# A two-layer gated cross-attention and mixture-of-experts block: Newton steps of seven layer norm chains on VectorE, and later gathers for chunks 5 to 7

## The chip, the cores and the metric

The kernel runs on one core of a Trainium2 chip. The metric is device time of one execution in microseconds, lower is better. The engines are named as the profile names them: PE (TensorE), DVE (VectorE), ACT (ScalarE), POOL (GpSimd) and SP (SyncE, which here issues DMAs). Each engine works through its own instructions strictly in the order in which they are written, and waits on semaphores for the others.

## The reference, cut to what matters

There are 32 sequences of 128 rows with 128 features, and two layers. Each layer is a cross-attention over 120 context rows with 16 heads, and a mixture of 8 experts of which each row takes two. Ahead of each of the four stands a layer norm without weights.

```python
def _layernorm(x, axis=-1, eps=1e-05):
    m = jnp.mean(x, axis=axis, keepdims=True)
    v = jnp.var(x, axis=axis, keepdims=True)
    return (x - m) / jnp.sqrt(v + eps)
...
x = x + jnp.tanh(g_xattn[0]) * _L0_xattn_ref(_layernorm(x, axis=-1), ctx_1024, ctx_1024, fside_BxSxS2_0, mask, ...)
x = x + jnp.tanh(g_ffn[0]) * _L0_ffn_ref(_layernorm(x, axis=-1), ...)
x = x + jnp.tanh(g_xattn[1]) * _L1_xattn_ref(_layernorm(x, axis=-1), ctx_1024, ctx_1024, mask, ...)
x = x + jnp.tanh(g_ffn[1]) * _L1_ffn_ref(_layernorm(x, axis=-1), ...)
```

The experts of layer 0 have a capacity: each row is sent to a place in its expert's table, the experts run over the tables, and the results are gathered back to the rows. The experts of layer 1 have none; each expert runs over all rows and its result is weighted.

## The kernel before

**Tiling.** The 32 sequences (rows 0 to 31 of `x_rows`, each 128x128) are worked in 8 chunks of 4 (`NCH`, `CB`). A chain of a layer norm is named by two numbers, `(who, n)`: `who` is 0 ahead of an attention and 1 ahead of the experts, `n` is the chunk, with 8 added in layer 1. Chunk 1 of layer 1, `n` = 9 (`HALVED`), is done in two halves of two rows each.

**The slots.** An attention is a walk over slots `s` = 0 to 139 or so: four per row, and in each a group of four heads passes through scores (PE), maxima (DVE, L986), exponentials (ACT, L805), their turn (PE, L529), the copy of the turned ones (DVE, L996 or L998; ACT takes one in four in layer 1), and later the weighted sums (PE, L542). Everything else is put by hand between these, by tables of offsets: `NEAR1`, `MID1`, `FAR1` and `FAR2` say at which slot of layer 1 the next chunk's statistics (`stat`), its root (`power`), its normalising (`norm`), its turn on PE (`turn`), its projection and the split of its queries stand; `POST` and `TIGHT0` say the same for what follows an attention chunk, the routing of the experts among it. DVE carries out, in a slot, first its `early` part, then its attention part, then its `behind` part. POOL has only `behind` and one small copy (L1426) every fourth slot.

**A layer norm chain.** DVE makes the statistics (L968, L972). POOL adds the epsilon (L1390), takes the power of minus one half (L1392), and refines it by one Newton step in four operations, then makes the shift `-m*r` in two (L1395 to L1405). Then the rows are normalised, `x*r + (-m*r)`, by POOL (L1418) or, for seven chains, by DVE (L1116): `(0, 8)`, both halves of `(0, 9)`, `(0, 10)`, `(0, 11)`, `(1, 6)` and `(1, 7)`. PE turns them (L463). In all seven, the slot of `norm` is later than the slot of `power`, by two or three; the chains `(0, 8)` and the first half of `(0, 9)` lie in the expert stage of layer 0.

**The gathers.** POOL also sends the rows to the tables (L1480, layer 0, `send`) and asks for the results (L1499, `bring`): two gathers a row, one in each of two slots, starting with slot `bring_slot(i)`. DVE adds them to the row at slot `add_y_slot(i)` (L1101, L1103), with rows 16 to 19 at slots 29 to 32, 20 to 23 at 38 to 41, 24, 25, 26, 27 at 50, 52, 54, 56 and 28 to 31 at 66, 68, 70, 72. The gathers of rows 24 to 27 began at slots 37, 39, 41, 43, those of rows 28 to 31 at 52, 54, 56, 58.

**The keys.** Behind the attention of layer 0, DVE splits the keys of layer 1 into three bf16 parts (L1165, L1167, L1169), for key chunks 0 and 1 at offset 2 of the last chunk, for chunk 2 at offset 5. `norm` of `(1, 7)` stands at offset 4, the logits (L1028) at 13. The experts of layer 0 begin when the last of the sends has landed.

Of the kernel before, what the change touches and what calls it, by code (L numbers as in the profile page):

```python
# [19 lines left out]
CB = 4  # L20
# [83 lines left out]


class Waits:

# [48 lines left out]
def bring_slot(i):  # L156

    c, b = divmod(i, CB)
    return {8: 0, 9: 7, 10: 9, 11: 11}[i] if c == 2 else {3: 13, 4: 21, 5: 29, 6: 37, 7: 52}[c] + 2 * b

# [28 lines left out]

SPLIT_KEYS_AT = {2: (0, 1), 5: (2,), 19: (3, 4, 5)}  # L190

# [26 lines left out]
def flamingo(nc, t, out, scratch):  # L218
# [193 lines left out]
    def ln_slot(who, n):  # L412
        return 0 if who == 0 else 1 + n % 2
# [540 lines left out]
    def vector_program(dve):  # L954
# [144 lines left out]
        def add_y(i):  # L1099
# [3 lines left out]
            dve.scalar_tensor_tensor(x[:, i, :], got[:, i % RING_Y, 1, :], slot_w[:, 1, i:i + 1], x[:, i, :], ALU.mult, ALU.add).then_inc(combine, 1)  # L1103

        def normalise_rows(who, n, c, h=0):
            if who:
# [8 lines left out]
            for b in part_of(None if who else n, h)[1]:  # L1115
                dve.tensor_scalar(xn[:, ln_slot(who, n), b, :], x[:, c * CB + b, :], rs[:, who, 2, b:b + 1], rs[:, who, 3, b:b + 1], ALU.mult, ALU.add).then_inc(ln_norm[who], 1)  # L1116

# [69 lines left out]
        def behind(l, s):  # L1187
# [11 lines left out]
            for P in range(1, NCH):  # L1199
                o, C, at = s - start_slot(l, P), l * NCH + P, prep_at(l, P)  # L1200
                if o == at["stat"]:
                    stat_rows(0, C, l, P)
                if l == 1 and P in ON_DVE1:
                    if o == at["norm"]:
                        normalise_rows(0, C, P)
# [6 lines left out]
            for j in range(NCH):  # L1212
                o, n = s - after_slot(j), l * NCH + j
                if o == post_at(l, j)["stat"]:
                    stat_rows(1, n, l, j)
                if l == 0 and j >= ON_DVE and o == post_at(l, j)["norm"]:
                    normalise_rows(1, j, j)
# [61 lines left out]
        def experts0():  # L1279
# [3 lines left out]
            for n in range(NJ):  # L1283
# [6 lines left out]
                if n == ADD_LAST:  # L1290
                    add_y(CB - 1)
                    stat_rows(0, NCH, 1, 0)
                if n == NORM_FIRST:
                    normalise_rows(0, NCH, 0)
                if n == SPLIT_FIRST:
# [3 lines left out]
                if n == ADD_NEXT:  # L1299
                    for i in range(CB, EARLY_ROWS):  # L1300
                        add_y(i)
                    stat_rows(0, HALVED, 1, 1, 1)
                if n == NORM_NEXT:
                    normalise_rows(0, HALVED, 1, 1)
# [72 lines left out]
    def gpsimd_program(pool):  # L1377
# [5 lines left out]
        def powers(who, n, h=0):  # L1383
# [7 lines left out]
            on.wait_ge(power, 2 * m + 1)  # L1391
            pool.tensor_tensor(r_s[:, 0, :], r_s[:, 4, :], half_c[:, 0:p], ALU.pow).then_inc(power, 1)  # L1392
            y, t_, r, m_r = (r_s[:, j, :] for j in range(4))
            on.wait_ge(power, 2 * m + 2)
# [528 lines left out]
```

## Time and profile before

| what | value |
|---|---|
| median of three runs | 959.44 us (957.41 to 962.17) |
| the profiled execution | 961.64 us |
| its span | 959.8 us |
| busy: PE, DVE, ACT, POOL | 793.3, 670.6, 608.5, 571.8 us |
| mean granted clock of PE | 0.941 of 2.4 GHz |

The span runs from the first to the last instruction; 1.8 us of the profiled execution lie around it. The stages are: attention of layer 0 up to 300 us, routing and keys up to 333, experts of layer 0 up to 463, attention of layer 1 up to about 730, experts of layer 1 to the end. The bracket at the end of a row of the view in order of time is the time for which the engine stood idle ahead of the instruction, and what ended it; a row without one began when the engine was free. Engines overlap neighbouring instructions a little, so what counts is from start to start.

### The profile page before, as it was taken

Reading aid. Unit: us, or ns where it says so; the run is one execution under the profiler, and the core shown is the slowest. Engines: PE = TensorE matmul, PEld = TensorE weight load, DVE = VectorE, ACT = ScalarE, POOL = GpSimd, SP = SyncE. Lnnn points to the kernel's source line nnn. Section 1 sums busy time; section 2 is a strip of 40 time slices with the busy share of each in tenths; the row PEclk is TensorE's granted clock in tenths of the full one; section 3 lists DMA queues with packets and bytes.
Section 4 is the critical chain, followed back from the end, with each engine's and each line's share of the span. In section 5 each row is a group of like instructions: output and inputs, shape, how many; then the busy total and the mean of one; then the engine's idle time right before and its main releaser. Section 6 shows DMA issues by size and latency. Waiting matters only on the chain.

```text
span 959.8 us, 20423 instructions
## 1 busy us (share of the span) xinstructions
PE 793.3 (83%) x6554; PEld 627.5 (65%) x6554; DVE 670.6 (70%) x1933; ACT 608.5 (63%) x2582; POOL 571.8 (60%) x872
## 2 busy tenths in 40 slices
PE   2268898988886399999876788788986889999996
PEld 1146666766664299998555556656765767888885
DVE  1246889999896534436688799998896575666664
ACT  1366888998982255444787678889996344444442
POOL 6364567888777500223477887574341767777775
PEclk9978999999996699999999889999998899999998
DMA  7929789536633742322537367454300000000000
GB/s 172 243 87 242 197 218 274 138 98 157 128 86 130 259 138 83 85 82 85 110 85 140 72 127 173 112 109 120 89 13 24 22 23 23 21 15 14 8 12 22
DMA packets 83699, 101.68 MB, mean 106 GB/s; under 512 B 8289, under 2 KB 69926, under 8 KB 82665
## 3 DMA queue, kind: packets, MB, share of 16 engines
q1 hardware_dynamic: 79496, 92.13, 37.4%
q0 software_dynamic: 4096, 8.25, 3.5%
q8 instruction: 52, 0.85, 0.4%
q14 instruction: 55, 0.44, 0.2%
HBM read 63.32 MB, written 45.99 MB: 114 GB/s over the span
## 4 chain that ended last, share of the span: by engine, by line
PE 41%; DVE 22%; ACT 14%; POOL 9%; issue 9%; DMA 5%; SPq 0%; POOLq 0%; ACTq 0%; DVEq 0%
ACT exp L805 10%; PE psum L654 7%; PE psum L691 5%; PE psum L693 5%; PE psum L692 5%; DVE shift L986 5%; DVE exp_T L996 2%; PE psum L542 2%; PE psum L529 2%; PE psum L642 2%; DVE ln_stats L968 2%; PE psum L643 2%; PE psum L644 2%; DVE exp_T L998 2%; PE psum L707 1%
## 5 line engine op out<-in xcount | busy, mean ns | idle before, releaser
L805 ACT ACTIVATE exp<-psum,shift 128x120 f32<-128x120 f32 x1024 | 364.8, 427 | 92.9 <-DVE shift L986 92.5
L805 ACT ACTIVATION_READ_ACCUMULATOR exp<-psum,shift 128x1 f32 x1024 | 269.8, 273 | 0.0
L986 DVE TENSOR_REDUCE shift<-psum 128x4 f32<-128x480 f32 x256 | 164.9, 646 | 55.4 <-PE psum L520 54.8
L529 PE MATMUL psum<-ident,exp 128*120 128x128 f32 x1024 | 164.5, 285 | 35.1 <-DVE exp_T L998 22.0
L1569 POOL TENSOR_TENSOR q_operand<-q_operand 128x512 f32<-128x512 f32 x96 | 125.9, 1311 | 70.3 <-DVE q_operand L1345 66.1
L1345 DVE SCALAR_TENSOR_TENSOR q_operand<-psum,comb,q_operand 128x256 f32<-128x256 f32 x256 | 111.7, 479 | 79.9 <-ACT q_operand L933 79.9
L529 PEld LDWEIGHTS psum<-ident,exp 128*120 128x120 f32 x1024 | 120.4, 143 | 53.9 <-DVE exp_T L998 26.5
L933 ACT ACTIVATE q_operand<-psum 128x512 f32<-128x512 f32 x128 | 76.4, 598 | 122.3 <-PE psum L693 122.2
L1499 POOL DMA_INDIRECT got_rows<-scratch_y,slot_get x64 | 66.9, 1046 | 121.9 <-DMA scratch_y<-y_rows 104.5
L517 PE MATMUL psum<-neg_rows,const_bf 128*128 128x480 bf16 x256 | 98.7, 386 | 48.4 <-ACT exp L805 27.5
L691 PE MATMUL psum<-w_T_high,xn_T_high 128*128 128x512 f32 x256 | 108.8, 425 | 9.5 <-DVE w_T_low L1311 7.3
L693 PE MATMUL psum<-w_T_high,xn_T_low 128*128 128x512 f32 x256 | 102.5, 400 | 0.0
L692 PE MATMUL psum<-w_T_low,xn_T_high 128*128 128x512 f32 x256 | 102.1, 399 | 0.0
L520 PE MATMUL psum<-k_operand,q_operand 128*128 128x240 bf16 x512 | 98.2, 275 | 0.0
L996 DVE TENSOR_TENSOR exp_T<-psum,group_T 120x512 f32<-120x512 f32 x128 | 85.1, 666 | 1.2 <-PE psum L529 1.2
L517 PEld LDWEIGHTS psum<-neg_rows,const_bf 128*128 128x128 bf16 x256 | 26.6, 104 | 79.7 <-ACT exp L805 49.8
L520 PEld LDWEIGHTS psum<-k_operand,q_operand 128*128 128x128 bf16 x512 | 51.7, 101 | 37.9 <-issue 10.9
L542 PE MATMUL psum<-exp_T,v_spread 120*32 120x128 f32 x2048 | 75.3, 292 | 0.7 <-POOL v_spread L1426 0.7
L1480 POOL DMA_INDIRECT scratch_xe<-xn_rows,slot_put x64 | 64.9, 1014 | 18.5 <-issue 17.4
L654 PE MATMUL psum<-w,q_operand 128*128 128x128 f32 (+1 forms) x576 | 69.1, 275 | 0.0
L654 PEld LDWEIGHTS psum<-w,q_operand 128*128 128x128 f32 (+1 forms) x576 | 66.9, 184 | 1.6 <-issue 0.7
L998 DVE COPY exp_T<-psum 120x512 f32<-120x512 f32 x96 | 65.2, 679 | 0.7 <-PE psum L529 0.7
(164 smaller groups left out, 1557.5 us busy)
## 6 DMA issues: line engine op xcount, KB each, us to landing
k_operand<-scratch_k SPq DMA_DIRECT2D x32, 360.0 KB, 6.3
q_operand<-scratch_q SPq DMA_DIRECT2D x30, 384.0 KB, 6.1
scratch_q<-parts SPq DMA_DIRECT2D x15, 384.0 KB
scratch_k<-parts SPq DMA_DIRECT2D x14, 360.0 KB, 5.2
scratch_xe<-in_zero_rows SPq DMA_DIRECT2D x8, 512.0 KB, 12.6
scratch_y<-in_zero_rows SPq DMA_DIRECT2D x8, 512.0 KB, 6.9
scratch_q<-parts SPq DMA_DIRECT2D x15, 256.0 KB
scratch_k<-parts SPq DMA_DIRECT2D x14, 240.0 KB, 5.3
```

Of the source, the lines that this page charges most:

```text
L517: pe.matmul(bank, ident_b, atts[l].neg[:, k, bb:bb + 1, :].broadcast_to([S, 4, S2]), start=True, stop=False)
L520: ins = pe.matmul(bank[:, 2 * u:2 * u + 2, :], qop[:, C % RING, pt, b * S:(b + 1) * S], kop[:, C % RING, pt, :, b * S2:(b + 1) * S2], star ...
L529: ins = pe.transpose(ps[0:S2, T_BANKS[G % 2], u * S:(u + 1) * S], atts[l].expS[:, G % RING_E, u, :], ident[:, :])
L654: ins = pe.matmul(bank[0:r_, s_ * D:(s_ + 1) * D], hT[:, n % 2, q, s_ * 128:s_ * 128 + r_], w2[:, e_, q, :], start=(q == 0), stop=(q == NC ...
L691: pe.matmul(bank, xh[:, c % 2, rows], vh[:, e_, :], start=True, stop=False)
L692: pe.matmul(bank, xh[:, c % 2, rows], vl[:, e_, :], start=False, stop=False)
L693: pe.matmul(bank, xl[:, c % 2, rows], vh[:, e_, :], start=False, stop=True).then_inc(f_up, 1)
L805: ins = act.activation(atts[l].expS[:, G % RING_E, u, :], ps[:, S_BANKS[G % 3], u * S2:(u + 1) * S2], ACT.Exp, bias=atts[l].shift[:, i % 2 ...
L986: dve.tensor_reduce(atts[l].shift[:, i % 2, 4 * r:4 * r + 4], ps[:, S_BANKS[G % 3], 0:4 * S2].rearrange("p (h k) -> p h k", h=4), AX_X, AL ...
L996: dve.tensor_tensor(dst, src, att0.gT[:, c % 2, b:b + 1, :].broadcast_to([S2, 4, S]), ALU.mult).then_inc(taken_v, 1)
L1345: dve.scalar_tensor_tensor(dst[:, half], ps[:, 2 * (w % R_UP) + k, 0:HID1], comb[:, c, b, 2 * p + k:2 * p + k + 1], sg[:, w % R_SG, half], ...
L1569: pool.tensor_tensor(acc[:, i % R_ACC, :], acc[:, i % R_ACC, :], ga[:, m % R_GA, :], ALU.add).then_inc(f_sum, 1)
```

## The change

The last part of the root moves to DVE for the seven chains whose rows DVE normalises. POOL still adds the epsilon and takes the power, and then stops; six operations of it go away in each chain. DVE gets three: `t = y*y`, `t = (v*-0.5)*t`, `r = (t+1.5)*y`. The shift `-m*r` goes away: the rows are normalised as `(x-m)*r`, in one operation of the same shape.

The new function `roots` waits for POOL's power. It is called at the slot of `power`, not at that of `norm`. In the expert stage it stands directly ahead of the normalising of `(0, 8)`, and directly behind the statistics for the first half of `(0, 9)`.

The gathers of chunk 5 are asked for one slot later (from slot 30), those of chunk 6 eight slots later (from 45), and those of chunk 7 eight slots later (from 60). The slots at which DVE adds them stay. The splits of keys 0 and 1 go from offset 2 to 5, behind the normalising of `(1, 7)`, and those of key 2 from 5 to 8.

```diff
+NEWTON_ON_DVE = [(0, NCH), (0, NCH + 1), (0, NCH + 2), (0, NCH + 3), (1, NCH - 2), (1, NCH - 1)]
+
+def newton_on_dve(who, n):
+    return (who, n) in NEWTON_ON_DVE
...
-    return {8: 0, 9: 7, 10: 9, 11: 11}[i] if c == 2 else {3: 13, 4: 21, 5: 29, 6: 37, 7: 52}[c] + 2 * b
+    return {8: 0, 9: 7, 10: 9, 11: 11}[i] if c == 2 else {3: 13, 4: 21, 5: 30, 6: 45, 7: 60}[c] + 2 * b
...
-SPLIT_KEYS_AT = {2: (0, 1), 5: (2,), 19: (3, 4, 5)}
+SPLIT_KEYS_AT = {5: (0, 1), 8: (2,), 19: (3, 4, 5)}
...
+        def roots(who, n, h=0):
+            p = CB // 2 if h else CB
+            r_s, m_v = rs[:, who, :, 0:p], mv[:, who, 0:p, :]
+            power, rstd, m = (h_pow, h_rstd, 0) if h else (ln_pow[who], ln_rstd[who], n)
+            y, t_, r, v = (r_s[:, j, :] for j in (0, 1, 2, 4))
+            on.wait_ge(power, 2 * m + 2)
+            dve.tensor_tensor(t_, y, y, ALU.mult).then_inc(rstd, 1)
+            on.wait_ge(rstd, 6 * m + 1)
+            dve.scalar_tensor_tensor(t_, v, -0.5, t_, ALU.mult, ALU.mult).then_inc(rstd, 1)
+            on.wait_ge(rstd, 6 * m + 2)
+            dve.scalar_tensor_tensor(r, t_, 1.5, y, ALU.add, ALU.mult).then_inc(rstd, 4)
...
-                dve.tensor_scalar(xn[:, ln_slot(who, n), b, :], x[:, c * CB + b, :], rs[:, who, 2, b:b + 1], rs[:, who, 3, b:b + 1], ALU.mult, ALU.add).then_inc(ln_norm[who], 1)
+                dve.tensor_scalar(xn[:, ln_slot(who, n), b, :], x[:, c * CB + b, :], mv[:, who, b, 0:1], rs[:, who, 2, b:b + 1], ALU.subtract, ALU.mult).then_inc(ln_norm[who], 1)
...
                 if l == 1 and P in ON_DVE1:
+                    if o == at["power"]:
+                        roots(0, C)
                     if o == at["norm"]:
                         normalise_rows(0, C, P)
...
+                if l == 0 and j >= ON_DVE and o == post_at(l, j)["power"]:
+                    roots(1, j)
                 if l == 0 and j >= ON_DVE and o == post_at(l, j)["norm"]:
                     normalise_rows(1, j, j)
...
                 if n == NORM_FIRST:
+                    roots(0, NCH)
                     normalise_rows(0, NCH, 0)
...
                     stat_rows(0, HALVED, 1, 1, 1)
+                    roots(0, HALVED, 1)
...
             pool.tensor_tensor(r_s[:, 0, :], r_s[:, 4, :], half_c[:, 0:p], ALU.pow).then_inc(power, 1)
+            if newton_on_dve(who, n):
+                return
```

Where it moves instructions, first DVE in the attention of layer 1, chain `(0, 11)`, slots 24 to 26, before:

```order
L972 BN_AGGR ln_mean_var<-ln_stats 128x2 x4
L986 TENSOR_REDUCE shift<-psum 128x4
L998 COPY exp_T<-psum 120x512
L1023 SCALAR_TENSOR_TENSOR x_rows<-psum,tanh_g_xattn,x_rows 128x512
L986 TENSOR_REDUCE shift<-psum 128x4
L1003 RECIPROCAL inverse<-den 128x16
L1009 COPY inverse_spread<-inverse 128x128
L1116 TENSOR_SCALAR xn_rows<-x_rows,ln_rstd 128x128 x4
```

and with the change (`L980` is `L972` of before, `L994` is `L986`, `L1137` is `L1116`):

```order
L980 BN_AGGR ln_mean_var<-ln_stats 128x2 x4
L1120 TENSOR_TENSOR ln_rstd<-ln_rstd 128x4
L1122 SCALAR_TENSOR_TENSOR ln_rstd<-ln_rstd 128x4
L1124 SCALAR_TENSOR_TENSOR ln_rstd<-ln_rstd 128x4
L994 TENSOR_REDUCE shift<-psum 128x4
L1006 COPY exp_T<-psum 120x512
L1031 SCALAR_TENSOR_TENSOR x_rows<-psum,tanh_g_xattn,x_rows 128x512
L994 TENSOR_REDUCE shift<-psum 128x4
L1011 RECIPROCAL inverse<-den 128x16
L1017 COPY inverse_spread<-inverse 128x128
L1137 TENSOR_SCALAR xn_rows<-x_rows,ln_mean_var,ln_rstd 128x128 x4
```

The three root steps stand directly behind the statistics, so two maxima, one copy of turned exponentials and one addition of the attention's output, which stood ahead of the first wait for POOL, now stand behind it.

Second DVE behind the attention of layer 0, chain `(1, 7)`, before (L1165 to L1169 are the splits of keys, L1133 ends the routing of chunk 6):

```order
L1133 TENSOR_TENSOR slot_weight<-r_gate,r_tmp 128x4 x2
L1165 TENSOR_TENSOR full<-full,parts 128x480
L1167 CAST parts<-full 128x480
L1169 TENSOR_TENSOR parts<-full,parts 128x480
L1165 TENSOR_TENSOR got_rows<-got_rows 128x480
L1167 CAST got_rows<-got_rows 128x480
L1169 TENSOR_TENSOR got_rows<-got_rows 128x480
L1116 TENSOR_SCALAR xn_rows<-x_rows,ln_rstd 128x128 x4
L1165 TENSOR_TENSOR full<-full,parts 128x480
```

and with the change:

```order
L1154 TENSOR_TENSOR slot_weight<-r_gate,r_tmp 128x4 x2
L1120 TENSOR_TENSOR ln_rstd<-ln_rstd 128x4
L1122 SCALAR_TENSOR_TENSOR ln_rstd<-ln_rstd 128x4
L1124 SCALAR_TENSOR_TENSOR ln_rstd<-ln_rstd 128x4
L1137 TENSOR_SCALAR xn_rows<-x_rows,ln_mean_var,ln_rstd 128x128 x4
L1186 TENSOR_TENSOR full<-full,parts 128x480
L1188 CAST parts<-full 128x480
L1190 TENSOR_TENSOR parts<-full,parts 128x480
L1186 TENSOR_TENSOR got_rows<-got_rows 128x480
```

The normalising has moved ahead of all three splits of keys; before, it stood behind two of them.

Third POOL in the attention of layer 1, slots 28 to 31, from the end of the chain `(1, 8)` to the normalising of its rows, before (L1499 is a gather, L1448 adds a bias):

```order
L1405 TENSOR_TENSOR ln_rstd<-ln_rstd 128x4
L1499 DMA got_rows<-scratch_y,slot_get 128x128
L1448 TENSOR_TENSOR x_rows<-x_rows,bo_rows 128x512
L1499 DMA got_rows<-scratch_y,slot_get 128x128
L1448 TENSOR_TENSOR x_rows<-x_rows,bo_rows 128x512
L1499 DMA got_rows<-scratch_y,slot_get 128x128
L1418 TENSOR_SCALAR xn_rows<-x_rows,ln_rstd 128x128 x4
```

and with the change:

```order
L1434 TENSOR_TENSOR ln_rstd<-ln_rstd 128x4
L1477 TENSOR_TENSOR x_rows<-x_rows,bo_rows 128x512
L1528 DMA got_rows<-scratch_y,slot_get 128x128
L1477 TENSOR_TENSOR x_rows<-x_rows,bo_rows 128x512
L1528 DMA got_rows<-scratch_y,slot_get 128x128
L1447 TENSOR_SCALAR xn_rows<-x_rows,ln_rstd 128x128 x4
```

One gather of three is gone from ahead of the normalising.

## Rows read from the trace of the kernel before

**Rows 1.** The page, the chain of work that ended last, by engine.

```profile
PE 41%; DVE 22%; ACT 14%; POOL 9%; issue 9%; DMA 5%; SPq 0%; POOLq 0%; ACTq 0%; DVEq 0%
```

**Rows 2.** Stretches of layer 1: length, busy time and count by engine, clock, DMA.

```profile
490.00:530.00 40.00, 27.71 (x294) 20.75 (x290) 32.60 (x91) 27.73 (x141) 30.34 (x49) 0.91 0.63 121
530.00:560.00 30.00, 22.35 (x196) 16.36 (x184) 24.77 (x60) 20.87 (x101) 25.92 (x39) 0.84 0.39 94
```

**Rows 3.** DVE in order of time, end of layer 0: start, length, engine, line.

```profile
283.71 0.62 DVE L986 TENSOR_REDUCE shift<-psum 128x4 f32<-128x480 f32 x1
...
289.65 1.12 DVE L1116 TENSOR_SCALAR xn_rows<-x_rows,ln_rstd 128x128 f32<-128x128 f32 x4 [1.94 <-POOL ln_rstd L1405]
```

**Rows 4.** POOL in order of time, the two chains at the end of layer 0.

```profile
286.83 1.05 POOL L1392 TENSOR_TENSOR ln_rstd<-ln_rstd,minus_half 128x4 f32<-128x4 f32 x1
...
302.92 1.05 POOL L1392 TENSOR_TENSOR ln_rstd<-ln_rstd,minus_half 128x4 f32<-128x4 f32 x1
...
318.36 0.97 POOL L1480 DMA_INDIRECT scratch_xe<-xn_rows,slot_put  x1 [1.03 <-DVE slot_weight L1133]
```

**Rows 5.** DVE in order of time, behind the attention of layer 0.

```profile
304.60 0.65 DVE L1165 TENSOR_TENSOR full<-full,parts 128x480 f32<-128x480 f32 x1
...
308.01 1.11 DVE L1116 TENSOR_SCALAR xn_rows<-x_rows,ln_rstd 128x128 f32<-128x128 f32 x4
...
313.00 0.19 DVE L1028 COPY r_logits<-psum 128x32 f32<-128x32 f32 x1 [2.18 <-PE psum L563]
```

**Rows 6.** DVE in order of time, attention of layer 1.

```profile
473.89 0.62 DVE L986 TENSOR_REDUCE shift<-psum 128x4 f32<-128x480 f32 x1
...
475.38 0.42 DVE L1142 TENSOR_TENSOR full<-full,parts 128x256 f32<-128x256 f32 x1 [0.27 <-ACT parts L777]
...
491.59 0.66 DVE L978 TENSOR_TENSOR v_rows<-psum,bv_rows 120x512 f32<-120x512 f32 x1
...
495.15 1.14 DVE L1116 TENSOR_SCALAR xn_rows<-x_rows,ln_rstd 128x128 f32<-128x128 f32 x4
...
502.35 1.50 DVE L1101 SCALAR_TENSOR_TENSOR x_rows<-got_rows,slot_weight,x_rows 128x128 f32<-128x128 f32 x1
...
511.51 0.63 DVE L986 TENSOR_REDUCE shift<-psum 128x4 f32<-128x480 f32 x1
...
516.24 1.11 DVE L1116 TENSOR_SCALAR xn_rows<-x_rows,ln_rstd 128x128 f32<-128x128 f32 x4 [1.86 <-POOL ln_rstd L1405]
...
529.50 0.35 DVE L1101 SCALAR_TENSOR_TENSOR x_rows<-got_rows,slot_weight,x_rows 128x128 f32<-128x128 f32 x1 [3.65 <-DMA got_rows<-scratch_y,slot_get]
...
532.49 0.35 DVE L1101 SCALAR_TENSOR_TENSOR x_rows<-got_rows,slot_weight,x_rows 128x128 f32<-128x128 f32 x1 [0.48 <-DMA got_rows<-scratch_y,slot_get]
```

**Rows 7.** POOL in order of time, attention of layer 1.

```profile
474.39 1.04 POOL L1392 TENSOR_TENSOR ln_rstd<-ln_rstd,minus_half 128x4 f32<-128x4 f32 x1
...
492.09 1.05 POOL L1392 TENSOR_TENSOR ln_rstd<-ln_rstd,minus_half 128x4 f32<-128x4 f32 x1
...
502.42 1.26 POOL L1448 TENSOR_TENSOR x_rows<-x_rows,bo_rows 128x512 f32<-128x512 f32 x1
...
513.43 1.05 POOL L1392 TENSOR_TENSOR ln_rstd<-ln_rstd,minus_half 128x4 f32<-128x4 f32 x1
...
519.50 1.01 POOL L1499 DMA_INDIRECT got_rows<-scratch_y,slot_get  x1 [0.30 <-issue]
...
535.35 0.25 POOL L1390 TENSOR_SCALAR ln_rstd<-ln_mean_var 128x4 f32<-128x4 f32 x1
```

**Rows 8.** PE in order of time, the turn of chunk 4.

```profile
543.46 0.97 PE L463 MATMUL psum<-ident,xn_rows 128*128 128x128 f32 x4 [1.96 <-POOL xn_rows L1418]
```

**Rows 9.** The gathers of L1499 from 460 to 700 us, issue to landing.

```profile
DMA to landing us min/median/max: 2.5/2.9/10.7
```

**Rows 10.** DVE in order of time, two small steps, each waiting for the last.

```profile
576.42 0.19 DVE L1093 TENSOR_TENSOR comb_work<-comb_work,r_onehot 128x32 f32<-128x32 f32 x1
576.64 0.19 DVE L1095 TENSOR_TENSOR comb<-comb_work,comb_sum 128x32 f32<-128x32 f32 x1
```

## The prediction

> **What bounds the kernel now.** I read the chain of work that ended last first. There the reader is to see that no engine has the path alone: PE holds 41% of it, DVE 22%, ACT 14%, POOL 9% [rows 1]. The change touches DVE and POOL, which pass the path to and fro in short pieces. Then the busy time by stretch. In the attention of layer 1, from 490 to 530 us, DVE is busy 32.6 of 40 us and POOL 30.3; from 530 to 560 DVE has 24.8 of 30 and POOL 25.9 [rows 2]. So where three of the chains stand DVE is the fuller one, and behind them POOL is. Then DVE and POOL in order of time, at each of the seven chains: what stands idle ahead of the normalising, and when POOL's power ends.
>
> **What the root costs.** On DVE the three steps are small and each waits for the last. Two such steps stand 0.22 us apart [rows 10], so the three take about 0.6 us, with what follows. On POOL six operations go away: the power of chain (0, 11) runs until 513.43 + 1.05 = 514.48, and the normalising that waits for the sixth begins at 516.24 [rows 6, 7], so some 1.7 us a chain, 12 in all. But that is not the main term. The root now stands at the slot of the power, directly behind the statistics, and DVE stops there until the power is through; the power alone takes 1.05 us, and POOL may be late. What is queued behind the stopped DVE are maxima, for which ACT's exponentials wait, and copies of turned exponentials, for which PE waits.
>
> **A, chain (1, 6), end of layer 0.** The operation behind the statistics starts at 283.71; the power ends at 286.83 + 1.05 = 287.88 [rows 3, 4]. The root ends at about 288.45. The work that stood between, 289.65 - 1.94 - 283.71 = 4.00 us, follows, so normalising begins at 292.45 instead of 289.65 [rows 3]: +2.8. Maxima and copies of turned exponentials are in that work, so PE and ACT are held too; I take it whole.
>
> **B, chain (1, 7) and the keys.** The routing ahead ends at 304.60 [rows 5], and the power at 302.92 + 1.05 = 303.97 [rows 4], so the root waits for nothing. Root 0.65, normalising 1.02, then the splits of three keys at (308.01 - 304.60) / 2 = 1.7 each: 5.1. The sum is 311.4, where the logits began at 313.00 after 2.18 us of idle for PE [rows 5]. PE's part of them comes 1.7 x 2 - 0.65 earlier, at 310.3, so DVE sets the start: -1.6. The sends of the last chunk stand behind the routing (those of chunk 6 waited 1.03 us for it [rows 4]), so this reaches the experts.
>
> **The expert stage, (0, 8) and half of (0, 9):** nothing. DVE only waits for PE there, and 0.6 us goes into that idle.
>
> **C, other half of (0, 9).** The next maximum moves from 473.89 to 474.39 + 1.04 + 0.6 = 476.03 [rows 6, 7]: 2.1 us, less the idle of 0.27 close behind [rows 6]: +1.8.
>
> **D, (0, 10).** From 491.59 to 492.09 + 1.05 + 0.6 = 493.74; the normalising at 495.15 had no idle ahead to give back [rows 6, 7]: +2.15.
>
> **E.** Until then POOL's additions of the bias met DVE's additions of the experts' results: at 502.35 one took 1.50 us, beside POOL's at 502.42; alone it takes 0.35, as at 529.50 [rows 6, 7]. With DVE 3.9 us later and POOL not, the two part: -1.15.
>
> **F, (0, 11).** From 511.51 to 514.48 + 0.6 = 515.08, +3.57; the normalising no longer idles for 1.86 [rows 6, 7]: +1.7.
>
> **G, the gather of row 18 and the turn of chunk 4.** DVE stood 3.65 us for a gather at 529.50 and 0.48 for the next at 532.49 [rows 6]. POOL asks for these in a run behind the chain (0, 11), one at 519.50 [rows 7]. By C to F (1.8 + 2.15 - 1.15 + 1.7) DVE comes 4.5 us later to its addition. The run starts with POOL's power, which moves by the 2.8 us of C to E, less the 1.7 that POOL saves: +1.1. So most of the wait goes; with the 0.48, DVE gets back 4.1. What is late next is the turn of chunk 4: PE waited 1.96 us at 543.46 for POOL's normalising [rows 8]. The chain of it began on POOL at 535.35 without idle, so behind POOL's queue [rows 7]. That queue is 1.7 us shorter by the chain and a gather shorter ahead of the normalising of (1, 8) (1.01 + 0.30 = 1.3 us [rows 7]), but the statistics, which DVE gives, now come at most half a us later than before, so I take only 0.3 of the 3. G is -4.4. Of the stops in C to F nearly nothing is left at the turn of chunk 4.
>
> **H, gathers of chunks 6 and 7.** They were asked for 13 slots before their use, and now 5, some 8 us. They land after 2.5 to 10.7 us, in the middle 2.9 [rows 9]; POOL can be late on top. From below: they no longer stand ahead of POOL's work at slots 37 to 44, and one or two additions of DVE that met POOL, each worth up to 1.50 - 0.35 us as in E, may pass alone: -1.8. From above: four rows that each wait up to 2 us at twice, 5 us after what idle is there already. I take the one at its middle landing, with a little of the other: +0.3.
>
> **The sum:** A 2.8, B -1.6, C 1.8, D 2.15, E -1.15, F 1.7, G -4.4, H 0.3 = +1.6 us. The profiled execution took 961.64, so 963.2; the median is 2.2 below it, so 961.0.
>
> **A rule against the sum.** POOL's row at 502.42 beside DVE's at 502.35 shows a DVE operation at four times its length [rows 6, 7]. The Trainium skill, page "SBUF — State Buffer", section "Who interferes with whom", says that a DVE instruction that reads two SBUF operands and a GpSimd instruction that reads SBUF lock each other out for the whole of one, and whoever is first has it. All three root steps have two such operands. By this rule a root step beside a POOL operation costs up to one POOL operation more. Here POOL issues gathers or nothing behind the power, so by the trace nothing is added; by the rule at its worst it would be, as an estimate from the row of 1.50, 1.15 us at each of five chains, 5.8 in all, and 967.
>
> **The rivals.**
> Late gathers (slower). The place is DVE's additions of rows 24 to 31 at slots 50 to 56 and 66 to 72. The price is the landing, up to 10.7 us [rows 9], less the lead of 8: 2.7 for the first of each group, and as much again where POOL asks late because of its own queue. It decides from a landing over 8 us behind the slot. For it: DVE stood 3.65 us at 529.50 with the lead of before. Against: the middle is 2.9. It gives +5 over the forecast, 966.
> All stops pass on (slower). C, D and F stand ahead of maxima on which ACT hangs. If the run of gathers moves with DVE's statistics by the whole 2.8 us and POOL's savings go into its own waits, the wait at 529.50 keeps 3.65 + 2.8 - 4.5 = 1.95 and the 0.3 at the turn falls away: +2.3, and up to +4.4 if the next gather's wait grows by as much. That is 963.3 to 965.4.
> The slack takes them (faster). PE and ACT work ahead by a group or two, and POOL, earlier by its savings, has the power of (0, 11) ready sooner than 1.9 us behind the statistics. Then A, C, D and F are worth half (8.45 / 2 = -4.2) and H is at its lower end (-2.1): 954.7, and 953.0 if one more of POOL's seven savings of 1.7 counts.
> That the change doesn't do what it says is no rival here: the order of the two shows the moves as written.
>
> **How the numbers follow.** About 0.5%, 4.8 us, is what a measurement of this kernel can tell from no change: 954.6 to 964.2. Forecast as summed, 958 to 964: 0.52. Late gathers: 0.14, with another 0.05 for the lock of the rule. All stops pass: 0.12, half of it over 964.2. The slack takes them: 0.17, most of it at 953 to 954.6, so 0.14 of it is faster and 0.03 is not. Faster is 0.14, slower 0.14 + 0.05 + 0.06 = 0.25, same 0.61. The range, to leave out 2 in 10 (the far ends of the slack and of the late gathers), reaches from 954.5 to 967.5.
>
> **What would show it.** In the changed profile, idle of DVE ahead of the first root step (L1120) of about 4.2 us at (1, 6), none at (1, 7), 1.5 at (0, 9) and (0, 10), 3.0 at (0, 11); the logits of the last chunk behind the splits, 1.6 us earlier against the end of the attention of layer 0; the addition at slot 30 without its wait of 3.65; PE's turn of chunk 4 no longer behind POOL; rows 24 to 31 added without idle for their gathers. The forecast is wrong if the waits for L1120 show up as no delay of the copies behind them, or if the additions at slots 50 and 66 wait for a DMA.

## The result, and the profile after

Twenty runs of each kernel: 966.12 us against 959.92, ratio 1.0063, 95% interval 1.0045 to 1.0080. The changed kernel is 0.63% slower. The forecast was 961.0; its range of 954.5 to 967.5 holds the time, but the likeliest case, a time within 0.5%, is not what happened. The time is that of the rival on late gathers, 966.

The profiled execution of the changed kernel took 963.22 us (span 961.4), 2.9 below the median of its kernel, and that of before 961.64, 1.7 above its own. So the two traces are only 1.6 us apart where the kernels are 6.2 apart. For this reason I read stages, not spans. The stages are cut at instructions that both kernels have: the last routing step ahead of the chain (1, 6), the two last copies of logits of layer 0 (L1028 before, L1036 after), the first split of the experts' rows, and the first and last maximum (L986, L994) of layer 1.

| stage | before, us | after, us | difference | forecast |
|---|---|---|---|---|
| start to routing of chunk 5 (nothing changed yet) | 283.62 | 282.60 | -1.02 | 0 |
| to the logits of chunk 6 (A) | 14.86 | 15.40 | +0.54 | +2.8 |
| to the logits of chunk 7 (B) | 14.52 | 12.93 | -1.59 | -1.6 |
| to the first rows in the experts | 21.17 | 20.45 | -0.72 | 0 |
| experts of layer 0 | 129.38 | 129.42 | +0.04 | 0 |
| attention of layer 1 (C to H) | 256.25 | 263.08 | +6.83 | +0.4 |
| the rest | 240.0 | 237.5 | -2.5 | 0 |

The first and the last row are not the change's doing as far as can be shown, nor is the fourth: the kernel of e2 below, whose code up to there is that of the changed kernel, takes 21.35 us for it, and e1 and e4 take 21.29 and 21.02. From the last maximum to the last expert step the profiled kernels that follow took between 228.8 and 231.6 us, whatever was changed ahead of it; before took 230.8 and after 228.3. Without these three rows the change makes +5.8, near to the 6.2 of the medians.

The busy time by stretch, after (columns as in [rows 2]):

```profile
490.00:530.00 40.00, 26.57 (x238) 19.79 (x229) 31.91 (x93) 26.31 (x132) 27.51 (x36) 0.79 0.56 114
```

From 490 to 530 us POOL has gone from 30.34 to 27.51 us, DVE from 32.60 to 31.91, and PE's granted clock from 0.91 to 0.79 [rows 2]. DVE was not made busier, it stands idle for POOL.

DVE in order of time at the end of layer 0, after; these rows answer to [rows 3, 5]:

```profile
286.90 0.16 DVE L1120 TENSOR_TENSOR ln_rstd<-ln_rstd 128x4 f32<-128x4 f32 x1 [4.13 <-POOL ln_rstd L1419]
...
291.37 1.11 DVE L1137 TENSOR_SCALAR xn_rows<-x_rows,ln_mean_var,ln_rstd 128x128 f32<-128x128 f32 x4
...
304.12 0.15 DVE L1120 TENSOR_TENSOR ln_rstd<-ln_rstd 128x4 f32<-128x4 f32 x1
...
310.93 0.18 DVE L1036 COPY r_logits<-psum 128x32 f32<-128x32 f32 x1
```

DVE stands 4.13 us for POOL's power at (1, 6) (L1120 is the first root step), none at (1, 7), and the logits of chunk 7 (310.93) follow the splits without idle, where they had waited 2.18 us for PE.

DVE in the attention of layer 1, after, which answers to [rows 6]:

```profile
473.03 0.16 DVE L1120 TENSOR_TENSOR ln_rstd<-ln_rstd 128x4 f32<-128x4 f32 x1 [1.50 <-POOL ln_rstd L1419]
...
492.70 0.16 DVE L1120 TENSOR_TENSOR ln_rstd<-ln_rstd 128x4 f32<-128x4 f32 x1 [1.49 <-POOL ln_rstd L1419]
...
504.12 0.66 DVE L994 TENSOR_REDUCE shift<-psum 128x4 f32<-128x480 f32 x1 [0.52 <-PE psum L528]
...
505.29 0.34 DVE L1109 SCALAR_TENSOR_TENSOR x_rows<-got_rows,slot_weight,x_rows 128x128 f32<-128x128 f32 x1
...
507.03 0.66 DVE L994 TENSOR_REDUCE shift<-psum 128x4 f32<-128x480 f32 x1 [1.01 <-PE psum L528]
...
517.22 0.16 DVE L1120 TENSOR_TENSOR ln_rstd<-ln_rstd 128x4 f32<-128x4 f32 x1 [2.79 <-POOL ln_rstd L1419]
...
520.58 1.11 DVE L1137 TENSOR_SCALAR xn_rows<-x_rows,ln_mean_var,ln_rstd 128x128 f32<-128x128 f32 x4
```

The three stops are 1.50, 1.49 and 2.79 us. A stop that the prediction didn't have, 1.15 us at the first half of (0, 9) in the expert stage, did not lengthen that stage. The normalising of (0, 11) at 520.58 no longer waits, and no DMA wait stands at slot 30. PE's turn of chunk 4, which answers to [rows 8]:

```profile
544.10 0.63 PE L471 MATMUL psum<-ident,xn_rows 128*128 128x128 f32 x4 [2.14 <-POOL xn_rows L1447]
```

It waited 2.14 us, against 1.96.

Where the start of each maximum lies against before, from the first one of layer 1 (-2.75 us) on: +2.3 at C, +2.6 at D, +0.9 at E, +1.5 at F behind its normalising, +0.7 ahead of the addition of row 18, then -5.0 up to the turn of chunk 4. That is 2.8 for C to G. From there to the end of the attention +4.1: that is H, and it comes in two steps, +2.7 at slot 54 and +4.5 between slots 66 and 72. DVE there, and POOL beside it:

```profile
583.28 1.39 DVE L1109 SCALAR_TENSOR_TENSOR x_rows<-got_rows,slot_weight,x_rows 128x128 f32<-128x128 f32 x1 [0.92 <-DMA got_rows<-scratch_y,slot_get]
584.70 1.29 DVE L1111 SCALAR_TENSOR_TENSOR x_rows<-got_rows,slot_weight,x_rows 128x128 f32<-128x128 f32 x1
...
613.05 1.99 DVE L1111 SCALAR_TENSOR_TENSOR x_rows<-got_rows,slot_weight,x_rows 128x128 f32<-128x128 f32 x1
...
617.93 0.53 DVE L1109 SCALAR_TENSOR_TENSOR x_rows<-got_rows,slot_weight,x_rows 128x128 f32<-128x128 f32 x1 [0.52 <-DMA got_rows<-scratch_y,slot_get]
618.50 2.88 DVE L1111 SCALAR_TENSOR_TENSOR x_rows<-got_rows,slot_weight,x_rows 128x128 f32<-128x128 f32 x1
...
624.91 0.35 DVE L1109 SCALAR_TENSOR_TENSOR x_rows<-got_rows,slot_weight,x_rows 128x128 f32<-128x128 f32 x1 [1.01 <-DMA got_rows<-scratch_y,slot_get]
```

```profile
613.72 1.16 POOL L1470 TENSOR_TENSOR parts<-full,parts 128x512 bf16<-128x512 f32 x1
...
617.69 1.01 POOL L1528 DMA_INDIRECT got_rows<-scratch_y,slot_get  x1 [0.30 <-issue]
618.71 0.30 POOL L1455 COPY v_spread<-v_rows 120x128 f32<-120x128 f32 x1
618.97 1.26 POOL L1588 TENSOR_TENSOR w_T<-w_T,w_last 128x512 f32<-128x512 f32 x1
620.19 1.03 POOL L1518 TENSOR_TENSOR bo_part<-bo_rows,comb_sum 128x512 f32<-128x512 f32 x1
```

Three rows wait 0.92, 0.52 and 1.01 us for gathers, and four additions that take 0.35 us alone take 1.39, 1.29, 1.99 and 2.88. Each of the four ends 0.14 to 0.16 us behind the end of an operation of POOL; the one of 2.88 (618.50 to 621.38) ends behind the second of two of 128x512 (620.19 + 1.03 = 621.22). The Trainium skill, page "SBUF — State Buffer", section "Who interferes with whom", says that such pairs, a DVE instruction with two operands in SBUF and a GpSimd instruction that reads SBUF, block each other for whole instructions; the trace agrees, and shows that one DVE instruction can be held through two of POOL's of 128x512 and a short copy ahead of them. Its row begins 0.21 us ahead of that copy (618.71), so here the one that began first, by the rows, was the one held.

How much of the delay these additions make can't be read from their length. From row 28 to row 31 DVE takes 17.60 us, where it took 13.85 before, and the whole difference lies in the last step, from row 30 to row 31: 6.98 us against 3.17. The addition of row 31 (624.91) waits for the last gather. That one stands at slot 67 on POOL, but POOL issued it at 617.69, when DVE was already at row 30 (slot 70), and DVE could go on 7.22 us later. Had the addition of 2.88 us been short, DVE would have stood there longer; e4 below shows this case.

### The profile page after: what moved, and what is told of

Same layout as the page of the kernel before. It is cut to its first block, busy times and chain, and to the rows that moved or that the text cites. A ratio compares the mean times of both kernels' runs of the same rounds, so it can differ in the third digit from the quotient of the medians.

```text
span 961.4 us, 20409 instructions
## 1 busy us (share of the span) xinstructions
PE 788.4 (82%) x6554; PEld 625.8 (65%) x6554; DVE 676.3 (70%) x1954; ACT 609.3 (63%) x2582; POOL 561.9 (58%) x830
## 4 chain that ended last, share of the span: by engine, by line
PE 39%; DVE 20%; POOL 12%; ACT 11%; issue 10%; DMA 5%; SPq 0%; POOLq 0%; DVEq 0%; ACTq 0%
ACT exp L813 8%; PE psum L662 7%; PE psum L699 5%; PE psum L701 5%; PE psum L700 5%; DVE shift L994 5%; DVE exp_T L1004 2%; POOL got_rows L1528 2%; PE psum L650 2%; DVE ln_stats L976 2%; PE psum L537 2%; PE psum L550 2%; PE psum L651 2%; PE psum L652 2%; PE psum L564 1%
## 5 line engine op out<-in xcount | busy, mean ns | idle before, releaser
L813 ACT ACTIVATION_READ_ACCUMULATOR exp<-psum,shift 128x1 f32 x1024 | 265.0, 267 | 0.0
L994 DVE TENSOR_REDUCE shift<-psum 128x4 f32<-128x480 f32 x256 | 165.7, 648 | 55.7 <-PE psum L528 54.8
L550 PE MATMUL psum<-exp_T,v_spread 120*32 120x128 f32 x2048 | 71.5, 282 | 0.7 <-POOL v_spread L1455 0.7
```

Source lines behind the costliest of these rows:

```text
L813: ins = act.activation(atts[l].expS[:, G % RING_E, u, :], ps[:, S_BANKS[G % 3], u * S2:(u + 1) * S2], ACT.Exp, bias=atts[l].shift[:, i % 2 ...
L994: dve.tensor_reduce(atts[l].shift[:, i % 2, 4 * r:4 * r + 4], ps[:, S_BANKS[G % 3], 0:4 * S2].rearrange("p (h k) -> p h k", h=4), AX_X, AL ...
```

## The experiments

Four groups were run, each group on a chip of its own, beside the kernel before: e1 to e4, e5 to e8, e9 to e11, and e12. The chips of e5 to e8 and of e12 are slower: the kernel before takes 979.62 and 978.31 us there, and 958.96 and 960.54 on the other two. Theory 1: the late gathers cost most, and the stops of DVE the rest. Theory 2: the stops of DVE at the power are the whole loss, and what stands at slots 54 and 70 is chance.

### Gathers alone (e1)

The kernel before, with one line of the change:

```diff
-    return {...}[i] if c == 2 else {3: 13, 4: 21, 5: 29, 6: 37, 7: 52}[c] + 2 * b
+    return {...}[i] if c == 2 else {3: 13, 4: 21, 5: 30, 6: 45, 7: 60}[c] + 2 * b
```

> The kernel before with the later gathers of chunks 5 to 7 alone; POOL makes all roots as before. Theory 1 (late gathers cost): in the trace of the changed kernel DVE loses some 4 us between slot 54 and slot 72 of layer 1, in waits for landings (0.92, 0.52, 1.01 us) and in additions that meet POOL (1.39, 1.29, 1.99, 2.88 us instead of 0.35). So +4 us against before, ratio 1.004, with waits of DVE for got_rows at rows 24 to 31. Theory 2 (the stops of DVE for POOL's power cost): 0 to -1 us, ratio 0.999 to 1.000.

Measured: 965.62 us against 958.96, ratio 1.0065 (1.0043 to 1.0086). In its trace the attention of layer 1 takes 261.11 us against 256.25, with waits for gathers of 0.64 and 2.31 us at slots 70 and 72 and additions of 1.77, 1.30, 1.99 and 2.88 us. From row 28 to row 31 it takes 18.90 us, 8.17 of them from row 30 to row 31. The late gathers alone cost as much as the whole change. Theory 2 falls.

### All but the gathers (e2)

The changed kernel with the line above as it was before.

> The changed kernel with the gathers of before: roots on DVE at the slot of the power, keys behind the normalising. Theory 1: the end of layer 0 gives 1.75 us and the attention of layer 1 up to the turn of chunk 4 takes 2.8, so +1 us against before, ratio 1.001, 4 to 5 us faster than the changed kernel. Theory 2: as slow as the changed kernel, +6 us, ratio 1.006.

Measured: 960.88 us, ratio 1.0021 (1.0002 to 1.0041). What is left of the change costs 0.2%, by an interval that only just leaves out none.

### Roots at the slot of the normalising (e3, e9), and with late gathers (e4)

```diff
-                    if o == at["power"]:
-                        roots(0, C)
                     if o == at["norm"]:
+                        roots(0, C)
                         normalise_rows(0, C, P)
...
-                if l == 0 and j >= ON_DVE and o == post_at(l, j)["power"]:
+                if l == 0 and j >= ON_DVE and o == post_at(l, j)["norm"]:
                     roots(1, j)
```

> As the one before (gathers of before), but for the attention of layer 1 and for (1, 6), (1, 7) the three root steps stand at the slot of the normalising, directly ahead of it, so that DVE does not stop for the power. Theory 1: the stops cost 2.8 us in layer 1 and some 0.5 at (1, 6), which go: -2 to -3 us against before, ratio 0.997. Theory 2 gives the same or more, 3 to 6 us faster than the kernel with roots at the power. If both are wrong and DVE's busy time decides, no difference to the kernel with roots at the power.

> The changed kernel with the root steps at the slot of the normalising, gathers late as changed. Theory 1: 4 us more than with the gathers of before, so +1 to +2 us against before, ratio 1.001 to 1.002. Theory 2: without the stops nothing is left to pay, -2 us, ratio 0.998.

> The kernel with roots at the normalising and the gathers of before once more, as the base for the two behind it: in the last group the kernel before took 979.6 us, 20 more than in the first, and this base was not among it. If the ratio of the first group holds, 0.996; if the gain is larger where the kernel before is slower, as the padded one (0.9948, with 2 us of padding) lets expect, 0.992 to 0.993.

Measured: e3 955.17 us, ratio 0.9960 (0.9938 to 0.9982); e4, on the same chip, 960.36 us, ratio 1.0010 (0.9991 to 1.0029); e9, the same kernel as e3 in another group, 953.24 us, ratio 0.9926 (0.9899 to 0.9953). DVE in e3:

```profile
289.44 1.12 DVE L1137 TENSOR_SCALAR xn_rows<-x_rows,ln_mean_var,ln_rstd 128x128 f32<-128x128 f32 x4
...
295.49 0.19 DVE L1036 COPY r_logits<-psum 128x32 f32<-128x32 f32 x1 [0.73 <-PE psum L571]
...
513.03 0.16 DVE L1120 TENSOR_TENSOR ln_rstd<-ln_rstd 128x4 f32<-128x4 f32 x1
...
513.70 1.18 DVE L1137 TENSOR_SCALAR xn_rows<-x_rows,ln_mean_var,ln_rstd 128x128 f32<-128x128 f32 x4
```

The kernel of e3 also has the splits of keys where the changed kernel has them. The root at (0, 11) (513.03) begins without idle, and the normalising stands 0.67 us behind. The first gain is at the end of layer 0: from the routing of chunk 5 to the logits of chunk 6 e3 takes 11.03 us and e9 10.96, where before takes 14.86, after 15.40 and e2 15.36. The normalising there begins 1.05 us sooner behind the routing than before (4.98 against 6.03 us), since DVE no longer waits for POOL's shift. The larger part, 2.8 us, lies behind the normalising, where PE kept its clock. In e3 PE stood 0.55 us for these rows, where it had stood 1.61 before, was still granted 1.00, and ran the 32 weighted sums ahead of the logits in 1.08 us, where before took 1.94 (their rows before stand under e7):

```profile
290.00:293.00 3.00, 1.44 (x17) 0.93 (x9) 2.93 (x9) 0.59 (x1) 2.37 (x4) 1.00 0.13 44
```

```profile
293.32 1.08 PE L550 MATMUL psum<-exp_T,v_spread 120*32 120x128 f32 x32
```

The attention of layer 1 takes 253.73 us in e3 and 254.00 in e9, 257.58 in e2, 256.25 before. The move of the Newton steps to DVE and that of the keys together are a gain of 0.4 to 0.7% once DVE doesn't stop for the power; no run parts the two. By the traces the way from the logits of chunk 6 to those of chunk 7, where the keys stand, is 1.5 us of it (13.05 us in e3, 13.06 in e9, 14.52 before).

With late gathers (e4) 5.2 us are lost again. DVE in e4, at rows 30 and 31:

```profile
612.61 0.35 DVE L1111 SCALAR_TENSOR_TENSOR x_rows<-got_rows,slot_weight,x_rows 128x128 f32<-128x128 f32 x1
...
619.36 0.35 DVE L1109 SCALAR_TENSOR_TENSOR x_rows<-got_rows,slot_weight,x_rows 128x128 f32<-128x128 f32 x1 [3.88 <-DMA got_rows<-scratch_y,slot_get]
```

Here the second addition of row 30 met no operation of 128x512 and took 0.35 us instead of 2.88. Nothing was won by it: the wait at row 31 became 3.88 us instead of 1.01, and from row 30 to row 31 it takes 7.14 us, from row 28 to row 31 17.74. So at chunk 7 the landing of the last gather, 7.36 us behind its issue (612.00), sets the time, and the blocked addition only fills a part of the wait.

### One stop alone (e8)

> Gathers of before; the roots of (1, 6) and (1, 7) at the slot of the power as changed, those of the attention of layer 1 at the slot of the normalising. It parts the two stops: between the kernel with roots at the power and that with roots at the normalising stand 5.7 us. If the stop at (1, 6) makes 4.3 us of it, as the way from the routing of chunk 5 to the logits of chunk 6 says (15.36 against 11.03 us), the ratio is 1.000 to 1.001; if the stops of layer 1 make it all, 0.996.

Measured: 976.87 us, ratio 0.9974 (0.9957 to 0.9992). This is another chip than that of e1 to e4, and the kernel without a stop did not run on it. So only the ratios can be set side by side: 0.9926 and 0.9960 without a stop, 0.9974 with the one at (1, 6), 1.0021 with all. They are too far apart for the same kernel to part the stops. The traces say that both cost, and about as much. At (1, 6), from the routing of chunk 5 to the logits of chunk 6, it is 4.3 to 4.4 us in e2 against e3 and e9. On this chip it is 21.26 us in e8 against 16.10 in e5, of which 1.4 is a longer idle of ACT without a releaser. In the attention of layer 1 it is 3.6 to 3.9 us in e2 against e3 and e9. That the one at (1, 6) makes 4.3 of 5.7 us, or that those of layer 1 make all, as the two readings of the expectation had it, is not borne out.

### Chunk 6 or chunk 7 late (e5, e6, e10, e11)

From e3, with `7: 60` alone (e5, e10) or `6: 45` alone (e6, e11).

> Roots at the slot of the normalising, gathers as before but for chunk 7, which are asked for eight slots later (60). The kernel with all three groups late lost 6.3 us against it over the attention of layer 1, of which by the starts of DVE's maxima 4 to 4.8 lie behind slot 66. Theory 1a (the price lies at each group's own additions): 4 to 5 us of loss here, ratio to before 0.996 + 0.0045 = 1.0005. Theory 1b (the price is a shift of POOL's work as a whole and needs all three groups): under 2 us, ratio 0.998 or less.

> The same with chunk 6 late alone (45 instead of 37). Theory 1a: 2 us of loss at slots 54 to 56, with some 1 of it given back at slots 41 to 48 where POOL has no gathers to issue, ratio 0.9975. Theory 1b: none, 0.996.

> As the base, with the gathers of chunk 7 late (60) alone. By the last group (0.9933 against 0.9948 for the padded base, which should be 2 us slower than the base) chunk 7 costs nothing: what DVE waits at slots 66 to 72 (4.1 us more in the trace) is given back at slots 50 to 66 (4.3 us less). So the base's ratio within 0.001. If theory 1a holds for chunk 7, 0.0045 above the base.

> As the base, with the gathers of chunk 6 late (45) alone. By the last group (0.9993) chunk 6 costs 5 us, more than the 2 us that its waits and long additions at slots 54 and 56 show: 0.005 above the base. If that was the one chip's, 0.002 above the base.

Measured: on the first slower chip e5 972.25 us, ratio 0.9933 (0.9916 to 0.9950), and e6 978.64 us, 0.9993 (0.9977 to 1.0010). In the group of e9 (953.24 us): e10 955.84 us, 0.9961 (0.9938 to 0.9984), and e11 955.97 us, 0.9957 (0.9933 to 0.9982). There each costs 2.6 to 2.7 us over e9, which adds up to the 5.2 between e4 and e3; but the intervals overlap that of e9 (0.9899 to 0.9953), so neither of the two is clear of noise by itself. On the slower chip chunk 6 costs 6.4 us more than chunk 7, and chunk 7 by the times nothing: e5 is 1.6 us quicker than e7, which has no late gathers and some padding. So the loss that theory 1a gave e5 (ratio 1.0005) was not there, while on the other chip e10 came out 0.0035 above its base, where 0.001 at most was expected and 0.0045 was the other case. How the price divides between the two chunks is open. DVE's additions of chunk 7 in e10 and, below, in its base e9:

```profile
608.49 0.35 DVE L1109 SCALAR_TENSOR_TENSOR x_rows<-got_rows,slot_weight,x_rows 128x128 f32<-128x128 f32 x1 [0.70 <-DMA got_rows<-scratch_y,slot_get]
608.88 2.88 DVE L1111 SCALAR_TENSOR_TENSOR x_rows<-got_rows,slot_weight,x_rows 128x128 f32<-128x128 f32 x1
...
615.42 0.35 DVE L1109 SCALAR_TENSOR_TENSOR x_rows<-got_rows,slot_weight,x_rows 128x128 f32<-128x128 f32 x1 [1.14 <-DMA got_rows<-scratch_y,slot_get]
```

```profile
606.55 1.41 DVE L1109 SCALAR_TENSOR_TENSOR x_rows<-got_rows,slot_weight,x_rows 128x128 f32<-128x128 f32 x1
```

With late gathers, two waits (0.70 and 1.14) and two blocked additions (1.99 and 2.88); in the base, one addition of 1.41. From row 28 to row 31 e10 takes 17.72 us and e9 13.85, which is +3.9; its whole attention of layer 1 takes 258.16 us against 254.00. In e5 it takes 17.77 us without the addition of 2.88, with a wait of 3.90 us at row 31: the same as in e4. Chunk 6 in e11:

```profile
580.79 0.49 DVE L1109 SCALAR_TENSOR_TENSOR x_rows<-got_rows,slot_weight,x_rows 128x128 f32<-128x128 f32 x1 [2.07 <-DMA got_rows<-scratch_y,slot_get]
```

DVE waits 0.19 us at row 24 and 2.07 at row 27 for a gather, and no addition of chunk 6 is blocked. From row 24 to row 27 it takes 16.08 us, and 13.58 in e9: +2.5. In the changed kernel it is 16.57, with two blocked additions and a wait of 0.92 us, against 13.57 in e2. So here too it comes out nearly the same, blocked or not. But the profiled execution of e11 was one of its quickest (span 951.4 us), and its attention of layer 1 takes 252.64 us, less than in e9: rows 28 to 31 take 12.38 us in it against 13.85. So these 2.5 us show where chunk 6 pays, and not that the whole is lost.

What made the slower chips slower can be named only in part. Their profiles have idle whose releaser is given as "remote", none of the core's engines, as in e5 on ACT; the profiles of before, after, e1 to e4 and e9 to e11 have none on PE, DVE and ACT:

```profile
300.79 0.59 ACT L756 COPY xn_T<-psum 128x512 f32<-128x512 f32 x1 [4.78 <-remote]
```

The copy of the turned chunk 6 stood 4.78 us, though PE had turned it. So a difference of 1 or 2 us in one stage of a profile from there says little.

### POOL padded (e7)

From e3, behind the power of (1, 6), on POOL:

```diff
+                if (who, n) == (1, NCH - 2):
+                    on.wait_ge(bo_done, 2)
+                    for k in range(3):
+                        pool.tensor_copy(bo_part[:], bo[:, 0:1, :].broadcast_to([S, CB, D])).then_inc(pad_done, 1)
+                        on.wait_ge(pad_done, k + 1)
```

> Roots at the slot of the normalising, but behind the power of chain (1, 6) POOL makes three copies of 128x512 that nobody needs, to fill the 1.7 us that the chain saved there. Theory V (in the last slots of layer 0 the path runs through POOL's spreading of V, which stands behind the chain and the sends, and on to PE's weighted sums): the logits of chunk 6 come 1.7 to 2.2 us later than with roots at the normalising, though DVE's normalising of (1, 6) stays where it was, and the time rises by as much, ratio 0.998. Rival (the path runs through DVE's normalising): the logits and the time stay, 0.996.

Measured: 973.89 us, ratio 0.9948 (0.9928 to 0.9968), on the first slower chip. POOL and DVE:

```profile
292.36 1.98 POOL L1423 COPY bo_part<-bo_rows 128x512 f32<-128x512 f32 x3
```

```profile
292.42 0.56 DVE L1120 TENSOR_TENSOR ln_rstd<-ln_rstd 128x4 f32<-128x4 f32 x1
...
293.71 1.47 DVE L1137 TENSOR_SCALAR xn_rows<-x_rows,ln_mean_var,ln_rstd 128x128 f32<-128x128 f32 x4
...
306.56 0.19 DVE L1036 COPY r_logits<-psum 128x32 f32<-128x32 f32 x1 [1.17 <-remote]
```

From the routing of chunk 5 to the logits of chunk 6 it takes 18.17 us, where e5 and e6 of that chip and e12 of the other slower one take 16.10, 16.07 and 16.10. The copies of 1.98 us cost 2.1. But 0.7 of it lies ahead of the normalising, where root steps beside the copies take 0.56 and 0.39 us instead of 0.16, and the four operations of the normalising take 1.47 us instead of 1.12, and in all four the way behind holds several us of idle without a releaser. The 2.1 us fit the theory that the path runs through POOL there, but the traces of the first chip don't show it: there the spreading of V (293.81 before) was over when PE reached the weighted sums (294.70). So the rival, that the way runs through DVE, explains at least half of the 2.1 us, and the point stays open.

What these traces do show is PE's clock. PE ahead of the logits of chunk 6, before and after, and DVE's wait for the sums before:

```profile
290.92 1.01 PE L463 MATMUL psum<-ident,xn_rows 128*128 128x128 f32 x4 [1.61 <-DVE xn_rows L1116]
...
294.01 0.77 PE L549 MATMUL psum<-ident,inverse_spread 128*128 128x128 f32 x2 [1.23 <-DVE inverse_spread L1009]
294.70 1.94 PE L542 MATMUL psum<-exp_T,v_spread 120*32 120x128 f32 x32
```

```profile
288.75 1.11 PE L537 MATMUL psum<-ident,exp 128*120 128x128 f32 x4 [5.05 <-DVE exp_T L1004]
...
295.89 1.08 PE L550 MATMUL psum<-exp_T,v_spread 120*32 120x128 f32 x32
```

```profile
296.71 0.29 DVE L1016 TENSOR_TENSOR o_T<-psum,inverse_rows 128x128 f32<-128x128 f32 x1 [2.85 <-PE psum L542]
```

The same 32 weighted sums take 1.94 us before and 1.08 after. The stretches (with 496 to 504, for the next section), before and after:

```profile
291.00:294.00 3.00, 1.78 (x8) 1.39 (x9) 2.17 (x6) 0.59 (x1) 2.39 (x4) 0.50 0.13 44
294.00:296.00 2.00, 1.99 (x29) 1.68 (x33) 0.00 (x0) 0.27 (x1) 1.52 (x3) 0.50 0.18 64
496.00:500.00 4.00, 3.56 (x19) 2.99 (x20) 2.68 (x8) 3.52 (x18) 3.21 (x5) 0.60 0.64 131
500.00:504.00 4.00, 4.00 (x53) 2.82 (x52) 3.96 (x7) 3.83 (x22) 3.53 (x5) 1.00 0.20 53
```

```profile
294.00:296.00 2.00, 0.99 (x11) 0.66 (x13) 1.02 (x3) 0.59 (x2) 1.70 (x2) 1.00 0.19 66
296.00:298.00 2.00, 2.00 (x41) 1.80 (x41) 0.29 (x2) 0.27 (x1) 0.97 (x2) 1.00 0.18 64
496.00:500.00 4.00, 1.95 (x10) 1.21 (x9) 3.28 (x10) 3.37 (x19) 3.39 (x5) 0.50 0.62 156
500.00:504.00 4.00, 4.00 (x19) 3.28 (x18) 2.81 (x5) 3.60 (x19) 3.23 (x3) 0.51 0.57 110
```

Before, PE is granted 0.50, the level of 1.2 GHz, from 291 us on, and had been idle for 1.61 us ahead of that and for 1.23 in it. After, it had been idle for 5.05 us during DVE's stop, was granted 0.50 behind that, and is back at 1.00 by the time of the weighted sums. So A's delay of 2.7 us on DVE was met by 2.2 us that the last part, from the normalising to the logits, ran faster (6.63 against 8.83). The trace of e2, which stops at the same place, has 1.00 and 1.08 us at the weighted sums too. It is no gain over having no stop, as e3 keeps 1.00 there without one.

### Half as late (e12)

From e3 with `6: 41, 7: 56`.

> Roots at the slot of the normalising, gathers of chunk 6 from slot 41 and of chunk 7 from slot 56, half as late as changed, so 9 slots ahead of their additions. If the landing is what costs (lead of 5 slots, some 8 us with POOL's own queue, against 2.7 us in the middle and 10 at most), 9 slots are enough: no wait of DVE for got_rows behind slot 48, row 28 to row 31 in 13.9 us as in the base, and the base's ratio (0.9926 to 0.996). If it is the place of the gathers on POOL (its additions of 128x512 come later and meet DVE's additions), rows 24 to 28 and 28 to 31 still take 1 to 4 us more than in the base, without a wait, and the ratio is 0.002 to 0.005 above it.

Measured: 972.97 us against 978.31, ratio 0.9954 (0.9933 to 0.9975), on the second slower chip. There is no wait for a gather behind slot 48. DVE's additions of rows 29 to 31:

```profile
620.44 1.21 DVE L1109 SCALAR_TENSOR_TENSOR x_rows<-got_rows,slot_weight,x_rows 128x128 f32<-128x128 f32 x1
...
624.89 1.14 DVE L1109 SCALAR_TENSOR_TENSOR x_rows<-got_rows,slot_weight,x_rows 128x128 f32<-128x128 f32 x1
626.07 1.31 DVE L1111 SCALAR_TENSOR_TENSOR x_rows<-got_rows,slot_weight,x_rows 128x128 f32<-128x128 f32 x1
```

Two rows still take 1.21 and 1.14 + 1.31 us: blocked without a wait. From row 28 to row 31 it takes 14.35 us, where e7 and e8, on the first slower chip, take 13.70 and 13.80 and e5 17.77. So the waits and the step of 4 us hang on the lead of 5 slots (4 at chunk 6), and 9 (8) are enough; some half a us of blocking stays with the place on POOL. The ratio can't tell: it lies within both expectations.

## Why the prediction held in part

**The cost of the root steps** is as worked out: 287.10 to 287.45 for the last two, 0.2 to 0.3 us a step. In the changed kernel POOL did not block them, as I took it against the worst case of the rule: 0.15 to 0.17 us each, but for two of 0.34 beside a gather's issue (473.50, 493.18). Beside POOL's copies in e7 two of them took 0.56 and 0.39, so the rule holds for them where POOL computes.

**A** was right on DVE and wrong on the path. DVE stood 4.13 us (4.17 forecast), and the normalising came 2.74 later against the routing ahead (2.8). The logits came only 0.54 later. The step that failed is "I take it whole": the profile of before showed DVE idle for 2.85 us for PE's weighted sums behind it, and PE ran them at half its clock.

**B** was right to 0.01 us.

**C, D and F** came out within half a us: +2.3, +2.6 and +1.5 against 1.8, 2.15 and 1.7.

**E** failed in sign. The collision went as forecast (505.29 takes 0.34 us, [rows 6] 1.50), but DVE waited 0.52 and 1.01 us for PE around it instead. From 496 to 504 PE was granted 0.50 and 0.51 where before it had 0.60 and 1.00: it had stood behind DVE's stop at D. I had costed the stop as time only, and not what PE's idle does to its clock.

**G** was right in size (-5.0 against -4.4), but for the turn: PE's wait of 2.14 us stayed, as POOL's chain there hung on DVE's statistics.

**H** is the term that was mis-sized: +0.3 forecast, +4.1 in the trace, and 5.2 to 6.7 us in the runs (e4 less e3, e1 less before). I knew both of its parts, and the step that failed is "I take the one at its middle landing". The row that decides is the last of a chunk. At row 31 DVE went on 7.2 to 8.5 us behind the issue of the last gather (five traces), and not 2.9; at row 27 of e11 it was 5.75. And POOL issued late, as the forecast had allowed but not priced: the last gather of row 31 came when DVE was three slots further than its place. A lead of 5 slots (4 at chunk 6, which I had also put at 5) was not enough for both. Why the last gather takes so long is open. In four of the five traces DVE goes on 0.9 to 1.0 us behind the end of the run of additions and copies that POOL does next, in e1 2.2, so it may hang on that work; no run tests it.

The other part, additions of DVE that meet POOL, did come, with up to 2.88 us for one. I had counted the meetings that would pass, and not those that would come. But with and without the longest of them the way from row 28 to row 31 takes 17.6 to 17.8 us on four traces, so at chunk 7 it lay inside the wait. Where no wait stands, in e12, the meetings cost half a us.

**The chances.** The late gathers had 0.14 and the price of 966; its mechanism, a landing later than the slot with POOL asking late, is what the traces show. That the time met 966 so closely is in part luck: the gathers cost up to 6.7 us, more than the 5 of that rival, and A cost 2.3 less than in the sum. The 0.52 for the sum rested on H.

## What to carry to other kernels

Work that is moved to another engine should be called where the result is wanted, not where it becomes possible: with the same root steps the kernel loses 0.2% at the slot of the power and gains 0.4 to 0.7% at that of the normalising. A transfer that is asked for later must be costed by its latest landing and not by the middle one, from the time at which the asking engine really comes to it. A long instruction ahead of a wait costs nothing by itself: look at what the time would be without it before it is called the cause. And two parts of a change that each have a sound reason are worth measuring apart: here one hid the other.

## What the runs showed of the hardware that I had not expected

A DVE instruction with two operands can be held through two POOL instructions in a row (2.88 us for one that takes 0.35). The last gather of a chunk asked for late let DVE go on only 5.8 to 8.5 us behind its issue, where the middle one took 2.9 to land [rows 9]. A pause of PE can give back a part of what it costs: a stop of 5 us, with its drop to 0.50 taken early, left 1.00 for the last 3 us of layer 0, where shorter pauses had left 0.50. And the kernel before took 959 to 961 us in three groups of runs and 978 to 980 in two others; even on two of the quicker chips the ratio of one kernel was 0.9960 (e3) and 0.9926 (e9).
